# Attention of one batch: scores in four row groups and four banks, the exponentials as the weights of the value product

## The reference

```
x = rmsnorm(layernorm(hidden), norm_w)
q, k, v = x @ wq.T, memory @ wk.T, memory @ wv.T          # 16 heads x 32
attn = softmax(where(mask, q k^T * 32**-0.5, -inf)), nan -> 0
out = (attn @ v) @ wo.T
x = x_in + tanh(g_xattn[0]) * sigmoid(x @ wg.T) * out
```

## Time and profile before

| | us |
|---|---|
| median of 3 runs | 1286.46 |
| lowest, highest | 1286.46, 1287.14 |
| the profiled execution, first to last instruction | 1286.6 |
| TensorE busy in it | 1210.8 (94%) |
| VectorE busy | 676.6 (53%) |
| ScalarE busy | 578.8 (45%) |
| GpSimd busy | 424.5 (33%) |

### The profile page before, as it was taken

The page is one execution under the profiler, slowest core; times in us unless marked ns, Lnnn a source line. Parts: engine busy times, 40 slices in busy tenths (PEclk is TensorE's granted clock), DMA queues, the critical chain, the costliest instruction groups (busy, mean ns, idle before and its releaser), DMA issues. The chain is left out here.

```text
span 1286.6 us, 25693 instructions
## 1 busy us (share of the span) xinstructions
PE 1210.8 (94%) x7835; PEld 1023.1 (80%) x7836; DVE 676.6 (53%) x1411; ACT 578.8 (45%) x1387; POOL 424.5 (33%) x514
## 2 busy tenths in 40 slices
PE   7998999999999879889999998999999999999995
PEld 7877777787787657667777777889999889999995
DVE  6656545545445989944576554642234552424241
ACT  5554445455356768872111112543344453434341
POOL 1102211211213656400015742244434334443443
PEclk9999999999999999989999999999999999999997
DMA  9100000000000122022000413764445766545454
GB/s 334 39 18 20 18 1 20 18 1 18 18 18 2 34 69 65 29 96 85 1 0 2 160 41 130 221 142 85 78 103 117 201 144 146 137 85 136 86 135 71
DMA packets 54335, 100.36 MB, mean 78 GB/s; under 512 B 5094, under 2 KB 21990, under 8 KB 54262
## 3 DMA queue, kind: packets, MB, share of 16 engines
q0 software_dynamic: 15824, 37.76, 15.5%
q1 hardware_dynamic: 38438, 61.65, 14.7%
HBM read 72.91 MB, written 26.48 MB: 77 GB/s over the span
## 5 line engine op out<-in xcount | busy, mean ns | idle before, releaser
L1925 PE MATMUL t_H<-m_W,t_xT 128*128 128x352 f32 x1632 | 281.9, 328 | 7.3 <-DVE m_W L2003 5.7
L1925 PEld LDWEIGHTS t_H<-m_W,t_xT 128*128 128x128 f32 x1632 | 263.3, 189 | 10.1 <-DVE m_W L2003 8.1
L1893 POOL DMA_INDIRECT out_dram<-t_ys,t_sid x68 | 109.5, 1610 | 225.0 <-ACT t_ys L1954 110.6
L1970 ACT ACTIVATE t_sl<-t_H 128x352 f32<-128x352 f32 x68 | 31.6, 465 | 175.6 <-PE t_H L1925 175.6
L759 ACT ACTIVATE pr<-SC,neg 128x128 f32<-128x128 f32 x256 | 90.1, 377 | 38.2 <-DVE neg L973 38.2
L47 PE MATMUL t_Y<-m_W,t_hT 128*128 128x512 f32 (+1 forms) x207 | 88.1, 426 | 4.9 <-issue 3.0
L2048 DVE TENSOR_TENSOR t_hT<-t_TH,t_hT 128x384 fp32r<-128x384 f32 x68 | 37.8, 556 | 101.8 <-ACT t_hT L1991 100.6
L2024 DVE TENSOR_TENSOR t_h<-t_H,t_sl 128x352 f32<-128x352 f32 x68 | 35.6, 523 | 104.8 <-ACT t_sl L1970 104.8
L1954 ACT ACTIVATE t_ys<-t_Y,t_wcol 128x512 f32<-128x512 f32 x69 | 47.4, 687 | 95.3 <-PE t_Y L49 95.3
L49 PE MATMUL t_Y<-m_W,t_hT 128*128 128x512 f32 (+1 forms) x207 | 82.5, 398 | 0.0
L48 PE MATMUL t_Y<-m_W,t_hT 128*128 128x512 f32 (+1 forms) x207 | 82.2, 397 | 0.0
(11 more groups left out here) (508 smaller groups left out, 3216.8 us busy)
## 6 DMA issues: line engine op xcount, KB each, us to landing
m_raw<-in_L_ffn_w_dram SPq DMA_DIRECT2D x28, 704.0 KB, 5.3
m_raw<-in_L_ffn_w_dram SPq DMA_DIRECT2D x14, 512.0 KB, 6.8
CT<-in_ctx_dram SPq DMA_DIRECT2D x8, 512.0 KB, 3.7
X<-in_x_dram SPq DMA_DIRECT2D x4, 1024.0 KB, 13.4
rows_d<-rows_first SPq DMA_DIRECT2D x16, 256.0 KB, 2.0
out_dram<-X SPq DMA_DIRECT2D x3, 1024.0 KB, 4.3
m_raw<-in_L_ffn_w_dram SPq DMA_DIRECT2D x14, 192.0 KB, 6.7
CT<-in_ctx_dram SPq DMA_DIRECT2D x8, 256.0 KB, 2.7
```

Source lines behind the costliest of these rows:

```text
L1893: pool.indirect_dma_start(out=m["out_rows"][:, :], out_offset=bass.IndirectOffsetOnAxis(ap=sid[:, b:b + 1], axis=0), in_=ys[:, b, :], in_o ...
L1925: x_ = pe.matmul(bk[b % 2][:, 0:I], xT[:, b % 2, jx, k, :], W13[:, jw, k, j, :], start=k == 0 and jx == jw, stop=k == KC - 1 and jx == 1)
```

## The change

The scores of a whole batch are one step `S`: four banks `SC`, one for each row group, with the heads of that row group in it; `O` and `REC` go. `sm.t` reads the bank of row group `t % 4`. The value product `pv` is now one projection-like step per batch into an `M` bank: the turned exponentials of a head (128x128) are the weights and the 32 columns of `va` move, so the result has a token per partition, and DVE divides it by a broadcast of the reciprocals over the free dimension. `bc` is now the four transposes of that result into a `T` bank, with ACT's copy to the high and DVE's subtraction to the low part; the steps `on` and `oT` go. `pT` has four tiles, `gs` one, `mrow` two. The order of the groups is written anew.

```diff
-        mrow = sb("mrow", [P, GB, S], BF16)
+        mrow = sb("mrow", [P, 2, S], BF16)
-        gs = sb("gs", [P, 2, D])
+        gs = sb("gs", [P, D])
-        pT = sb("pT", [P, 2, HQ, S])
+        pT = sb("pT", [P, HQ, HQ, S])
-        T, M, SC = bank("T", 2), bank("M", 2), bank("SC", 2)
-        O, REC = bank("O", 1)[0], bank("REC", 1)[0]
+        T, M, SC = bank("T", 2), bank("M", 2), bank("SC", HQ)
...
-                f"Sa.0 xT.2 Sb.0 sm.0 sm.1 v.0 st.-2 st.-1 cT.2 ra.-1 xT.3 {d[0]} g.0 rb.-1 pT.0 cT.3 q.1.0 rd.-1 Sa.1 pT.1 Sb.1 "
-                f"sm.2 sm.3 mk.4 q.1.1 u.-2 {d[1]} pv.0 q.1.2 sf.-4 sf.-3 pT.2 uT.-2 u.-1 {d[2]} q.1.3 Sa.2 pT.3 rc.0 Sb.2 sm.4 sm.5 "
-                f"fm.-2 bc.0 pv.1 on.0 oT.0 k.1.0 uT.-1 {d[3]} k.1.1 pT.4 {d[4]} v.1 fm.-1 Sa.3 pT.5 Sb.3 sm.6 sm.7 mk.5 "
...
+                f"S.0 pv.-1 sm.0 v.0 bc.-1 xT.2 xT.3 sm.1 pT.0 oP.-1 mk.1 {d[0]} g.0 pT.1 sm.2 q.1.0 st.-2 st.-1 cT.2 sm.3 ra.-1 q.1.1 "
+                f"cT.3 rb.-1 {d[1]} pT.2 q.1.2 rd.-1 {d[2]} pT.3 rc.0 q.1.3 u.-2 sf.-4 sf.-3 uT.-2 u.-1 fm.-2 "
+                f"S.1 pv.0 sm.4 v.1 bc.0 uT.-1 {d[3]} sm.5 pT.4 oP.0 mk.2 {d[4]} g.1 pT.5 sm.6 fm.-1 k.1.0 sm.7 k.1.1 nm.4 nm.5 pT.6 sf.-2 {d[5]} k.1.2 "
+                f"pT.7 rc.1 k.1.3 xT.4 sf.-1 "
+                f"S.2 pv.1 sm.8 v.2 bc.1 xT.5 cT.4 sm.9 pT.8 oP.1 mk.3 {d[6]} g.2 pT.9 sm.10 q.2.0 cT.5 st.0 sm.11 q.2.1 {d[7]} pT.10 q.2.2 "
+                f"nm.6 nm.7 pT.11 rc.2 q.2.3 "
+                f"S.3 pv.2 sm.12 v.3 bc.2 {d[8]} sm.13 oP.2 {d[9]} pT.12 st.1 mk.4 ra.0 g.3 pT.13 sm.14 rb.0 k.2.0 sm.15 rd.0 k.2.1 pT.14 u.0 k.2.2 "
+                f"pT.15 rc.3 uT.0 u.1 k.2.3 fm.0 uT.1 fm.1 ", g)
...
+            "S.2 pv.1 sm.8 v.2 bc.1 sm.9 pT.8 oP.1 mk.3 ta.0 tb.0 pT.9 sm.10 g.2 tc.0 sm.11 pT.10 an.0 qh.0 ks.0 st.0 "
+            "pT.11 rc.2 "
+            "S.3 pv.2 sm.12 v.3 bc.2 sm.13 oP.2 pT.12 st.1 ra.0 g.3 pT.13 sm.14 rb.0 sm.15 an.1 qh.1 ks.1 pT.14 rd.0 u.0 aS.0.0 "
+            "pT.15 rc.3 aT.0 pv.3 bc.3 aS.0.1 ag.0.0 aT.1 aS.0.2 ag.0.1 "
...
-        SPLIT, T_KINDS = ("xT", "cT", "aT", "rT"), ("xT", "cT", "aT", "rT", "pT", "uT", "ft")
-        BY_ACT, BY_DVE = ("q", "k", "g", "fg"), ("v", "oP", "fm", "aO")
+        SPLIT, T_KINDS = ("xT", "cT", "aT", "rT", "bc"), ("xT", "cT", "aT", "rT", "pT", "bc", "uT", "ft")
+        BY_ACT, BY_DVE = ("q", "k", "g", "fg"), ("v", "pv", "oP", "fm", "aO")
...
+                    elif kind == "pv":
+                        for h in range(NH):
+                            i = pe.matmul(bk[:, h * HD:(h + 1) * HD], pT[:, h % HQ, h // HQ, :], va[:, h, :], start=True, stop=True)
...
+                    elif kind == "bc":
+                        for j in range(KC):
+                            i = pe.transpose(bk[:, j * P:(j + 1) * P],
+                                             o[:, j * P:(j + 1) * P], identF[:, :])
...
+                        wait(pe, p_exp, HQ * t)
...
+                        for r in range(HQ):
+                            pe.matmul(SC[r][:, :].rearrange("p (j m) -> p j m", j=KC), c["onesB"][r * HD:r * HD + 1, :],
+                                      mrow[r * HD:r * HD + 1, t % 2:t % 2 + 1, :].to_broadcast([1, KC, S]), start=True, stop=False)
+                        for j in range(KC):
+                            for r in range(HQ):
+                                i = pe.matmul(SC[r][:, j * S:(j + 1) * S], qT[r * HD:(r + 1) * HD, t // 2 % 2, j, cols],
+                                              kT[r * HD:(r + 1) * HD, t // 2 % 2, j, cols], start=False, stop=j == KC - 1)
...
+                        dve.tensor_tensor(by_head(o[:, :]), by_head(M[(mf - 1) % 2][:, :]),
+                                          rec[:, t % 2, :].unsqueeze(2).to_broadcast([P, NH, HD]), ALU.mult).then_inc(m_dve, 1)
```

More of the change, by code:

```diff
@@ L298, in attention_and_ternary @@
             order[kinds] = {s: i + 1 for i, s in enumerate([s for s in plan if s[0] in kinds])}
-        for kinds in (SPLIT, T_KINDS, BY_ACT, BY_DVE, M_KINDS, X_UPD, STATS, PV):
+        for kinds in (SPLIT, T_KINDS, BY_ACT, BY_DVE, M_KINDS, X_UPD, STATS):
             order[kinds] = {s: i + 1 for i, s in enumerate([s for s in plan if s[0] in kinds])}
@@ L609, in _ @@
                         project(s, mf)
[L610 to L624, removed]
-                                          start=True, stop=False)
-                        else:
-                            pe.wait_ge(s_half, 2 * t + 2)
-                        for jj in range(2):
-                            for e, bk in enumerate(SC):
-                                r, slot = (2 * late + e) * HD, 2 * late + jj
-                                i = pe.matmul(bk[:, slot * S:(slot + 1) * S], qT[r:r + HD, b // 2 % 2, 2 * half + jj, cols],
-                                              kT[r:r + HD, b // 2 % 2, 2 * half + jj, cols], start=False, stop=slot == HQ - 1)
-                                if jj:
-                                    i.then_inc(s_fill if late else s_half, 1)
-                    elif kind == "pv":
-                        b, half = t // 2, t % 2
-                        pe.wait_ge(t_hi, at(T_KINDS, ("pT", 2 * t + 1)))
-                        if half == 0:
-                            pe.wait_ge(m_dve, at(BY_DVE, ("v", b)))
-                            wait(pe, o_norm, 2 * b)
-                        for jj in range(2):
-                            j = 2 * half + jj
-                            for r in range(HQ):
-                                i = pe.matmul(O[r * HD:(r + 1) * HD, j * S:(j + 1) * S], va[:, j * HQ + r, :],
-                                              pT[:, r % 2, r // 2 * 2 + jj, :], start=True, stop=True)
-                        i.then_inc(pv, 1)
-                    elif kind == "bc":
-                        pe.wait_ge(o_norm, 2 * t + 1)
-                        wait(pe, r_out, t)
@@ L689, in _ @@
                                 .then_inc(t_hi, 1)
+                        elif kind == "bc":
+                            wait(act, m_fill, at(M_KINDS, ("oP", t - 1)))
+                            act.activation(oT[:, 0, :, :].rearrange("p k t -> p (k t)"), src, ACT.Copy).then_inc(t_hi, 1)
                         elif kind in SPLIT:
@@ L753, in _ @@
                         wait(act, t_fill, at(T_KINDS, ("pT", t - 2)))
-                        wait(act, o_norm, 2 * (t // HQ) - 3)
+                        wait(act, o_norm, t // HQ - 1)
                         if t < 2:
@@ L912, in _ @@
                                           XT0[:, 0, :, t * P:(t + 1) * P].bitcast(F32), ALU.subtract).then_inc(t_lo, 1)
+                    elif kind == "bc":
+                        tf = at(T_KINDS, s)
+                        hi_, lo_ = (oT[:, h, :, :].rearrange("p k t -> p (k t)") for h in range(2))
+                        dve.wait_ge(t_hi, tf)
+                        dve.tensor_tensor(lo_, T[(tf - 1) % 2][:, :], hi_.bitcast(F32), ALU.subtract).then_inc(t_lo, 1)
                     elif kind in SPLIT:
@@ L938, in _ @@
                     elif kind == "mk":
-                        wait(dve, s_fill, 4 * (t - GB) + 4)
+                        wait(dve, s_fill, HQ * (t - 1))
                         dve.wait_ge(mg_in, 16 * (t // GB + 1))
-                        dve.tensor_scalar(mrow[:, t % GB:t % GB + 1, :], mask_g[:, t % GB:t % GB + 1, :],
+                        dve.tensor_scalar(mrow[:, t % 2:t % 2 + 1, :], mask_g[:, t % GB:t % GB + 1, :],
                                           -1.0, -MASKED, ALU.add, ALU.mult).then_inc(mrow_ready, 1)
@@ L945, in _ @@
                         dve.wait_ge(m_fill, mf)
-                        wait(dve, pv, at(PV, ("pv", 2 * t - 1)))
+                        wait(dve, m_fill, at(M_KINDS, ("pv", t - 1)))
                         dve.tensor_scalar(va[:, :, :], M[(mf - 1) % 2][:, :].rearrange("p (h d) -> p h d", h=NH),
```

100 lines of the change are left out of this document (41 added, 59 removed), and 12 rows, old and new, of the table d.

## The result

The kernel after takes 1358.24 us (median of four runs, 1357.10 to 1366.81) against 1286.80 for the kernel before on the same chip (four runs). The ratio is 1.056, with a 95% interval of 1.054 to 1.059: slower by 71 us, where the prediction had 33 and a range that ended at 1338.

The account below looks back on a forecast made before the run. TensorE's order of work was taken as the bound; stalls of the new order, 9.9 x 2 + 10 + 5 = +35 us on 1286.6, gave 1321, rounded down to 1320 us. Its own range was 1304 to 1336, with rivals 1284 to 1338.

Parts of the forecast that it names:

- TensorE's work: TensorE's own time per batch in the changed stage: 5.3 us after against 5.40, a gain of 1.6 us over 16 batches.
- cheap passes: Rival, value product: passes not bound by their weight load, 0.060 us each, 27 us less, 1293 us; chance 0.10.
- row groups in pairs: Rival, score block: the four row groups run two by two, 14 us more, 1334 us; chance 0.08.
- The order: Whole stage: TensorE stalls caused by the new order of steps, +9.9 us a steady group, +35 us in all.
- The walk: Step-by-step timing of each engine's queue over four batches of a steady group: 108.9 us, 12.9 of it idle.
- The quantiser: End of batch 0: VectorE's statistics steps and quantiser run to 29.0 us, TensorE is through at 26.65, idle 2.4 us.
- the bank of `bc`: Start of each batch: the next transposes wait for the copy and subtraction of this T bank, 1.1 to 1.5 us.
- the exponentials of batch 2: Batch 2: fourth exponentials end at 24.0 us while `pT.11` could start at 22.4, TensorE idle 1.6 us.
- the bank of cT in batch 0: Batch 0: cT.3's subtraction ends at 24.7 us, while `pT.3` is ready to run at 22.85; TensorE idle 1.9 us.
- more idle may also cost clock: All four groups: added TensorE idle may lower its clock, 2 us a group, up to 8 us, left inside the range.
- Near no change: Rival, whole stage: stalls of 8 us meet cheaper passes, 1287 us; chance 0.05.
- order free: Rival, whole stage: the new order costs nothing, idle stays 2.5 us a group, 1284 us, faster; chance 0.17.

Follow-up runs that it names:

- e1_wide: Kernel after with each value pass moving 128 columns of va (four heads) in place of 32, same plan and passes; 1330.1 us.
- e2_order: Kernel after with the plan alone rewritten: first two softmax steps before the previous batch's value product, two pT transposes and the v projection moved; 1318.5 us.
- e6: Only the change's scores, old value product once per batch into M banks, in the order of before with the halves merged; 1295.0 us.
- e3_oldpv: Kernel after with value product and reciprocal broadcast in their old form, per batch into M banks; scores and nearly all of the plan kept; 1305.4 us.
- e7_newpv_spaced: e6's plan with the change's value product of 32 moving columns, its transposes placed one projection behind the product; 1309.4 us.
- e10_wide_order2: The change's value product with 128 moving columns, in e9's plan with the transposes behind the next scores; 1321.8 us.
- e4_order_wide: Kernel after with both edits, e1_wide's 128-column value passes in e2_order's plan; 1301.3 us.
- e5: e3_oldpv's old-form value product and the change's scores, in e2_order's rewritten plan; 1311.6 us.
- e9: e6 with the plan alone changed: broadcast and value product of a batch stand before the next batch's scores; 1290.5 us.

## Why the prediction was wrong

The direction was right, the size was not: the loss is just over double the forecast.

**TensorE's work: right.** 3.60 for the product against 3.58, 1.3 for scores, 0.43 for the transposes. Thus the rivals of cheap passes and of row groups in pairs are out: the score block of 1.06 us less one length of 0.27 leaves seven steps of 0.11, the step of a pair in the earlier trace rows, with four instead of two. The Trainium skill, "TensorE: Matmul & The Clock Gate", Measured speedup vs the span model, has 3.07x for four row tiles of K=32, from which the prediction worked out 1.13 us for the 32 instructions. This trace doesn't agree: eight steps of 0.11 are 0.9 us, what eight pairs took.

**The order: right, and the size nearly.** The walk gave batches of 31.2, 24.7, 26.0 and 27.0 us, 108.9 together. e1_wide, where the clock is mostly restored, has 32.1, 25.1, 25.6 and 27.1: 109.9. (The terms named for batch 0 add up to 6.9 us, not to "some 6.5"; that changes nothing.) The waits are those of the walk. TensorE's own in a steady group of after, third group:

```profile
PE T L497 <- DVE fu L804: 2.4, 2, 2.2
...
PE M L509 <- ACT fuT L674: 2.2, 2, 1.3
...
PE T L497 <- ACT xT L666: 2.0, 2, 1.0
...
PE T L497 <- DVE cT L887: 1.8, 1, 1.8
...
PE M L47 <- DVE oT L881: 1.5, 1, 1.5
PE T L497 <- ACT pr L731: 1.5, 1, 1.5
```

The quantiser (2.4 forecast, 2.2 the longest here), its copy (0.9; 1.3), the bank of `bc` (1.1; 1.0), the output projection behind it (1.5; 1.5), the exponentials of batch 2 (1.6; 1.5, at 338.83 us) and the bank of cT in batch 0 (1.9; 1.8, at 276.24 us). Over the whole stage idle grew by 38 us in after and in e1_wide, and their rest columns, 31.4 and 32.8, stand for the forecast +35; e2_order took 27 of that back by a new plan alone. In e1_wide the first and last group together with what follows them lost 20.5 us where +15 was forecast (the first is shorter, as its last batch's product and `oP` are done in the next); some 22 of its 28.5 us at half clock lie there.

**The clock: the step that failed.** The sum had the order's +35 alone. The value passes stood in it by their own time, 3.6 us a batch, and nothing for what they do to the clock of the work around them; the only clock term, "more idle may also cost clock", up to 8 us, was left to the range. Measured: the short moving side costs 28 us in after's plan (e1_wide, where only the moving columns differ and idle is the same), 17 in e2's and 15 in e6's. The clock is at half for 85.3 us of the stage, against 9.6 before, which can cost (85.3 - 9.6)/2 = 38 us at most. The term for idle was small but not far off: at most 9.5 us in e1_wide, which has after's idle; at most 17.6 in e3_oldpv, which has no short pass. I had asked what a pass of this shape costs by itself, and found the right answer in the 16-column rows, but not what it does to the matmuls behind it.

The forecast 35 for the order and 0 to 8 for the clock of its idle thus stand against 42 in the stage of e1_wide (33 of rest, at most 9.5 of clock), and the forecast 0 for the short passes against 28. That the two make up the 71 is no further proof, since both are differences between the same three kernels. The evidence is that idle stayed when the passes were widened, and that busy time came back to 4 us over before's (485.0 and 481.0).

The price of the new product against the old depends on the order: 53 us in after's plan (e3_oldpv), 14 in e6's (e7_newpv_spaced), where the prediction had 1.8 us a batch, 29 in all.

**Near no change, order free:** out. The forecast's own test, a steady group under 101 us or `bc`'s bank waited for under 0.3 us, was not met by after.

Open: whether a plan exists in which the cheaper scores beat before. Two written by hand did not, and their forecasts were off by as much as the gain sought. Open too is what exactly the clock reacts to beside columns per load, and why six of after's value products have no fall: e10_wide_order2 and e3_oldpv show that idle has a share, and e4_order_wide that the two do not simply add.

## What to carry to other kernels

Price a matmul shape by its neighbours too: where each weight load is followed by few moving columns, look at the granted clock in the stretch behind it, in the nearest row of that kind, before counting only its step. When a result must pass through one more shared bank, walk each engine's queue from that bank's fill to its last reader; such a walk was right to 1 us in 109. The forecasts for e3, e5, e6 and e9, for which the record has no such walk, were 12 to over 40 us too low. And work taken from the busiest engine is only worth what its order lets through: 5 to 8 us a group less on TensorE brought nothing here, as the exponentials and the copies that free its banks share one queue.

## What was not expected of the hardware

- TensorE at full load of its weight path, PE and PEld busy 4.39 and 4.25 of 4.39 us, then went to half clock; with up to 128 instead of 32 columns, 4.46 and 4.33 of 4.46 us, it did not.
- 96 more moving columns per fp32 pass cost no time: 32 passes from start to next block are 3.60 us with 32 columns and 3.59 with 128.
- Four row groups of 32 rows run side by side at the step of two: 0.11 us for four instructions.
- The clock also falls with no short pass in the kernel: 44.9 us at half clock in e3_oldpv, 41.0 in e10_wide_order2 with wide passes. TensorE is idle in them for 76.8 and 66.2 us of the stage, 34.2 before.
